# A vision-transformer layer with routed experts on one core: weights loaded for the expert stage, the last image's routing and the place of the weighing runs rearranged

## The chip, the cores and the metric

One core of a Trainium2 chip runs the whole kernel. The metric is the device time of one execution in microseconds. A difference of about 0.3% (5.6 us) is what a measurement of this kernel can tell from no change.

## The reference

Eight images of 3x512x512 become 8x1024 tokens of 256 values. One attention layer with eight heads and a gate follows, then a feed-forward layer whose down projection is chosen per token.

```python
h = patches @ Wp + bp + pos                      # [8, 1024, 256]
# attention on layernorm(h), 8 heads of 32; the softmax's rows are queries,
# and its result is used transposed
attn = softmax(q @ k.T * 32 ** -0.5)
out  = einsum('bhij,bhid->bhjd', attn, v) * sigmoid(x @ Wg.T + bg)
h = h + x + out @ Wf.T + bf                      # x is the normed input
# routed layer on layernorm(h)
H = gelu(xf @ W1 + b1)                           # 1024 wide
probs = softmax(H @ Wr + br); e = argmax(probs)
h = h + probs[e] * (H @ Wd[e] + bd[e])
```

## The kernel before

The images go through a pipeline on five engines, each with its own queue, and every order is written out by hand in the functions `image` of each engine; semaphores tie them together.

**An image** is 64 steps, `G_STEPS` = 32 for each group of four heads. Step k = 4i + hh takes query tile i and head hh: TensorE (PE) makes 128x1024 scores in two matmuls (L561), VectorE (DVE) their maximum (L1219), ScalarE (ACT) the exponential with its row sum (L930). Two score buffers are in turn, so score k waits for exponential k - 2. After the fourth head of a tile `scale_v` divides the values by the row sums (L1028, L1031), and `weigh(b, i, j)`, j = 0 to 3, adds the tile's product with its exponentials to the output (L575, 16 matmuls for two j). `WEIGH_AT` puts j = 0, 1 in step 4i + 5 and j = 2, 3 in step 4i + 7, at the step's end. Eight exponential buffers are in turn; exponential k waits for the weighing of the group eight steps before.

**Between the scores** of image b run, by tables `*_AT` of steps, the rest of the projections of b, the embedding of b + 1 (L528, into the two spare banks, added by `embedded` on DVE), gates, transposes (`turn`), the first projections of b + 1 (`QK0_AT`), and the routing of b - 1 (`route`, 14 small parts on DVE, one of them reading `prefix`, two products on PE that count the tokens of each expert, L674 and L676; project (0, 0) waits until its bank is read, L1146). The router layer of b - 1 (`norm_turn`, `router`, L625 to L643) stands whole at step 32.

**SyncE's queue** (SP) carries, in order for image b, `load_stack(b, 0)`, the tiles of image b + 1, `load_stack(b, 1)`, `store_hidden(b - 1, u)` for four quarters and `store_prob(b - 1)` (L312, after parts 8 and 9 of the routing). `load_stack` copies the split queries and keys of a group into `st`, three transfers per head, when the group before has made all its scores.

**The expert weights**, 16 pieces of 128x1024, come in three stages: `load_down(m)` (SP, L319, four transfers into one of four raw buffers), `high_down(m)` (ACT, L878, rounds) and `split_down(m)` (GpSimd, that is POOL, L417, the rest). Load m waits for split m - 4. In image 7 ACT rounds pieces 0 to 3 at steps 44, 48, 52, 56; 4 to 8 follow once the last weighing is done, and 9 to 15 stand inside the last router, behind every second gelu. SP loads 0 to 9, and then two more behind each `store_hidden(7, u)`, which waits for four transposed pieces of the hidden layer.

**The end.** After image 7's attention: final projection (L612), sums on DVE (L1047), statistics, `root_3` on POOL (L382), `norm_3` (L1058), transposes (L625), the router's 16 hidden pieces (L633 to L635) with gelu (L891), logits (L643, L650), `route(7)`, `place` (POOL, L409, eight scatters of token numbers into a table in DRAM), a gather of the table, and then 71 slots of 128 tokens through the experts (L791, L803), some 283 us. `bd_parts`, the two parts of the expert bias, go to `bd` by 16 transfers of 1 KB.

## Time and profile before

| | us |
|---|---|
| median of 3 runs | 1850.87 (1847.99 to 1852.8) |
| the profiled execution | 1851.56 |
| its span, first to last instruction | 1849.7 |
| PE busy | 1630.2 (88%) |
| DVE busy | 1165.1 (63%) |
| ACT busy | 940.0 (51%) |
| POOL busy | 369.2 (20%) |

The page also cuts the span into 40 slices of 46 us. PE's busy tenths are 9 in nearly all; the exceptions are slices 1, 2 and 4, then slices 28 to 34 (1248 to 1572 us) with 8, 8, 6, 7, 3, 4, 3, and the last one. The granted PE clock reads 8 to 9 tenths or more in all but slices 31 to 34, which read 7, 7, 6, 5. The last column of a wait, [idle before <- releaser], says how long the engine stood idle and what ended it.

### The profile page before, as it was taken

The page shows a single profiled execution, that of the slowest core. Times are in us where ns is not written, and L with a number is a line of the kernel's source. Part 1 is how long each engine was busy: PE and PEld are TensorE (multiplying, and loading weights), DVE is VectorE, ACT ScalarE, POOL GpSimd, SP SyncE. Part 2 cuts the span into 40 slices and gives each one's busy share as a digit, 9 for nine tenths or more (in the row PEclk, how much of TensorE's full clock was granted, in tenths as well). Part 3 has the DMA queues.
Part 4 walks back from the last instruction along what each step waited for, and adds up shares of the span by engine and source line. Part 5 has one row for each costly group of instructions (what it writes and reads, how often), then busy time and mean ns, then how long its engine had stood idle before and what let it go on. Part 6 is the DMA issues. An engine that isn't in the chain of part 4 may idle for free.

```text
span 1849.7 us, 29190 instructions
## 1 busy us (share of the span) xinstructions
PE 1630.2 (88%) x10992; PEld 1116.3 (60%) x10992; DVE 1165.1 (63%) x1977; ACT 940.0 (51%) x1565; POOL 369.2 (20%) x296
## 2 busy tenths in 40 slices
PE   7796999999999999999999999998867343999998
PEld 6463556456646655665566466644433232999998
DVE  2377687767777776768687777767656512444443
ACT  0465565756575666557565756565555121222222
POOL 0202001210210021001202100210003323455553
PEclk9898999999999999999999999999987765999999
DMA  4313325241604351352426043512443253566663
GB/s 164 86 52 69 64 79 131 47 109 52 160 2 117 81 122 31 104 123 64 95 66 142 19 109 79 133 24 69 106 91 56 71 111 104 176 201 203 205 200 136
DMA packets 131378, 187.45 MB, mean 101 GB/s; under 512 B 22222, under 2 KB 96476, under 8 KB 131116
## 3 DMA queue, kind: packets, MB, share of 16 engines
q1 hardware_dynamic: 112828, 120.48, 27.5%
q0 software_dynamic: 17984, 63.81, 10.7%
q8 instruction: 92, 1.51, 0.3%
q10 hardware_dynamic: 432, 1.31, 0.2%
q14 instruction: 42, 0.34, 0.1%
HBM read 84.44 MB, written 51.68 MB: 74 GB/s over the span
## 4 chain that ended last, share of the span: by engine, by line
PE 69%; DVE 12%; issue 8%; ACT 4%; DMA 3%; SPq 2%; POOL 1%; POOLq 0%; ACTq 0%; DVEq 0%
PE ps L561 12%; PE ps L803 11%; PE ps L575 11%; PE ps L528 8%; DVE nmax L1219 6%; PE ps L791 3%; PE ps L612 3%; PE ps L633 3%; PE ps L549 3%; ACT pr L930 3%; PE ps L635 3%; PE ps L634 3%; PE ps L588 3%; PE ps L595 1%; PE ps L502 1%
## 5 line engine op out<-in xcount | busy, mean ns | idle before, releaser
L1219 DVE TENSOR_REDUCE nmax<-ps 128x1 f32<-128x1024 f32 x512 | 622.8, 1219 | 231.9 <-PE ps L561 226.7
L930 ACT ACTIVATE pr<-ps,nmax 128x1024 f32<-128x1024 f32 x512 | 570.0, 1113 | 304.9 <-DVE nmax L1219 291.1
L561 PE MATMUL ps<-st 96*128 96x512 f32 x1024 | 404.0, 479 | 76.8 <-ACT pr L930 67.7
L561 PEld LDWEIGHTS ps<-st 96*128 96x128 f32 x1024 | 171.0, 194 | 275.8 <-ACT pr L930 137.5
L575 PE MATMUL ps<-pr,vs 128*32 128x256 f32 x4096 | 279.4, 394 | 18.4 <-DVE vs L1031 16.0
L803 PE MATMUL ps<-wd,hg 128*128 x1704 | 222.7, 287 | 0.0
L803 PEld LDWEIGHTS ps<-wd,hg 128*128 128x128 f32 x1704 | 210.0, 192 | 0.0
L575 PEld LDWEIGHTS ps<-pr,vs 128*32 128x32 f32 x4096 | 110.9, 111 | 163.7 <-issue 80.9
L962 ACT ACTIVATE hg<-ps 128x512 fp32r<-128x512 f32 x142 | 77.3, 595 | 226.7 <-PE ps L791 226.7
L528 PE MATMUL ps<-wp,xt 128*128 128x256 f32 x672 | 172.8, 379 | 0.0
L891 ACT ACTIVATE ht<-ps,bf 128x512 f32<-128x512 f32 x128 | 87.9, 688 | 125.3 <-PE ps L635 125.3
L549 PE MATMUL ps<-nt,wqk 128*128 128x512 f32 x256 | 135.2, 614 | 7.1 <-DVE base L1146 3.6
L528 PEld LDWEIGHTS ps<-wp,xt 128*128 128x128 f32 x672 | 126.3, 189 | 24.8 <-DVE qk L1019 1.2
L409 POOL DMA_INDIRECT slot_table<-tid,addr_i x64 | 63.2, 988 | 369.4 <-DVE addr_i L1157 352.4
L633 PE MATMUL ps<-nt_high,wf 128*128 128x512 f32 x256 | 106.7, 417 | 32.6 <-ACT ht L891 31.0
L1302 DVE TENSOR_TENSOR hg<-ps,hg 128x512 fp32r<-128x512 f32 x142 | 91.6, 686 | 48.4 <-ACT hg L962 48.2
L372 POOL TENSOR_SCALAR vare<-mv 128x8 f32<-128x8 f32 x8 | 1.9, 236 | 515.5 <-DVE mv L989 515.5
L1309 DVE SCALAR_TENSOR_TENSOR rows<-ps,rows 128x256 f32<-128x256 f32 x71 | 34.3, 484 | 110.1 <-PE ps L805 110.1
L634 PE MATMUL ps<-nt_low,wf 128*128 128x512 f32 x256 | 103.5, 404 | 0.0
L635 PE MATMUL ps<-nt_high,wf 128*128 128x512 f32 x256 | 103.3, 403 | 0.0
L930 ACT ACTIVATION_READ_ACCUMULATOR pr<-ps,nmax 128x1 f32 x512 | 99.5, 194 | 0.0
L469 POOL DMA_INDIRECT out<-rows,slot_to x71 | 69.9, 985 | 122.8 <-DVE rows L1309 113.9
(131 smaller groups left out, 1836.2 us busy)
## 6 DMA issues: line engine op xcount, KB each, us to landing
st<-qk SPq DMA_DIRECT2D x192, 256.0 KB, 5.1
xt<-x_in SPq DMA_DIRECT2D x58, 384.0 KB, 3.1
token_rows<-staged_b SPq DMA_DIRECT2D x64, 256.0 KB, 4.8
token_rows<-staged_a SPq DMA_DIRECT2D x64, 256.0 KB, 4.8
token_rows<-hres POOLq DMA_DIRECT2D x8, 1024.0 KB, 5.3
wd<-w_down SPq DMA_DIRECT2D x64, 128.0 KB, 4.4
pr<-x_in SPq DMA_DIRECT2D x6, 384.0 KB, 9.7
rows<-token_rows,slot_from POOLq DMA_INDIRECT x71, 4.7
```

Of the source, the lines that this page charges most:

```text
L528: last = mm(spare(t)[:, 0:D], xt[:, t % 2, k, :], wp[:, k, :], start=(k == 0), stop=(k == KC - 1))
L549: last = mm(spare(j), wqk[:, c, w * D + g * P:w * D + (g + 1) * P], nt[:, c, hf * HALF:(hf + 1) * HALF], start=(c == 0), stop=(c == DC - 1))
L561: last = mm(ps[:, 2 * (k % SR) + j, :], stq[:, hh, i * P:(i + 1) * P], stk[:, hh, j * 512:(j + 1) * 512], start=True, stop=True)
L575: last = mm(ps[32 * hh:32 * hh + 32, O_BANK + j // 2, (j % 2) * D:(j % 2 + 1) * D], vs[:, gi % 2, hh, :], pr[:, (4 * gi + hh) % PR, j * D: ...
L633: mm(spare(bank), w_high, nt_high[:, c, half], start=(c == 0), stop=False)
L634: mm(spare(bank), w_high, nt_low[:, c, half], start=False, stop=False)
L635: last = mm(spare(bank), w_low, nt_high[:, c, half], start=False, stop=(c == DC - 1))
L803: mm(o, hg[:, s % 2, h_part, k, :], wd[:, bass.ds(e, 1), w_part, k, :], start=(k == 0 and h_part == w_part), stop=False)
L891: actv(ht[:, k, :], spare(bank), ACT.Gelu, bias=bf1[:, k:k + 1]).then_inc(S["ff_act"], 1)
L930: actv(pr[:, k % PR, :], ps[:, 2 * (k % SR):2 * (k % SR) + 2, :].rearrange("p a n -> p (a n)"), ACT.Exp, bias=nmax[:, k % 16:k % 16 + 1], ...
L1219: V.reduce_max(nmax[:, k % 16:k % 16 + 1], ps[:, 2 * (k % SR):2 * (k % SR) + 2, :].rearrange("p a n -> p (a n)"), AX_X, negate=True).then_ ...
L1302: V.tensor_tensor(hg[:, s % 2, 1, 4 * c:4 * c + 4, :].rearrange("p k n -> p (k n)"), ps[:, 2 * (s % 2) + c, :], high_part.bitcast(F32), AL ...
```

## The change

- **Weighing.** `WEIGH_AT` moves each pair one step later (4i + 6 and 4i + 8, at the end of a group 30 and 31), and `weigh` stands right behind the step's score, ahead of the other work of the step.
- **Prefix.** One step later (step 48) and into spare bank 1 instead of 0; the wait for its reading moves from project (0, 0) at step 49 to project (1, 0) at step 52.
- **Stacks.** Head hh's transfers wait only for that head's last score, so that the first may go three steps earlier.
- **Weight pieces.** SP loads 0 to 3 ahead of `store_prob(6)`, 4 to 13 ahead of the first `store_hidden(7, 0)`, 14 and 15 behind it. POOL splits 0 and 1 ahead of `place(6)`, and 2 to 6 ahead of `root_3(7)`; 7 on follow it. ACT rounds 4 to 9 ahead of the last router, 10 behind its four roundings, 11 to 15 behind gelus 2, 4, 6, 8, 10.
- **Last image in two halves.** `route` takes a unit: images 0 to 6 whole, image 7 as units 7 and 8 of four tiles. Unit 7's parts run between the block transposes of the router's second half (`HALF_AT`), its `prefix` behind hidden piece 5, its `place` (four scatters) behind the last split. Unit 8 follows as the whole did, with one scan part less and four scatters.
- **Bias.** Its rounding moves to step 58 of image 7, its split ahead of split 2; it goes out to DRAM in one transfer and back into `bd` in one.

```diff
-        PREFIX_AT = G_STEPS + 15
+        PREFIX_AT = G_STEPS + 16
+        HALF_PREFIX = 5
+        HALF_AT = {0: (0, 1), 1: (2, 3), 2: (4, 5), 3: (6,), 6: (10, 11), 7: (12, 13)}
         WEIGH_AT = {k: [(i, j) for i in range(15) if i != 7 for j in range(4)
-                        if k == min(4 * i + 5 + j // 2 * 2, (i // TILES + 1) * G_STEPS - 1)] for k in range(STEPS)}
+                        if k == min(4 * i + 6 + j // 2 * 2, (i // TILES + 1) * G_STEPS - 2 + j // 2)] for k in range(STEPS)}
...
                 hold(sp, "qk_lo", b * 8 + 4 * (g + 1))
-                hold(sp, "score_mm", b * STEPS + g * G_STEPS)
                 for hh in range(4):
+                    wait(sp, "score_mm", b * STEPS + g * G_STEPS - 3 + hh)
...
-            for m in range(8):
+            for m in range(4):
                 load_down(m)
-            load_down(8)
-            load_down(9)
+            store_prob(IMAGES - 2)
+            for m in range(4, 8):
+                load_down(m)
+            sp.wait_ge(S["bd_low"], 1)
+            sp.dma_start(bd_rows.rearrange("a e d -> e a d"), bd_parts.bitcast(F32)).then_inc(S["bd_out"], 16)
+            for m in range(8, 14):
+                load_down(m)
             store_hidden(IMAGES - 1, 0)
-            load_down(10)
-            load_down(11)
-            store_hidden(IMAGES - 1, 1)
-            load_down(12)
-            load_down(13)
-            store_hidden(IMAGES - 1, 2)
             load_down(14)
             load_down(15)
-            store_hidden(IMAGES - 1, 3)
+            for u in range(1, 4):
+                store_hidden(IMAGES - 1, u)
             store_prob(IMAGES - 1)
-            for part in range(2):
-                for e in range(EXPERTS):
-                    sp.dma_start(bd[part:part + 1, e, :].bitcast(F32), bd_parts[e:e + 1, part, :].bitcast(F32)
-                                 ).then_inc(S["bd_in"], 16)
+            sp.wait_ge(S["bd_out"], 16)
+            sp.dma_start(bd[0:2].bitcast(F32), bd_rows).then_inc(S["bd_in"], 16)
...
+                if not after:
+                    split_down(0)
+                    split_down(1)
                 if before:
-                    place(b - 1)
+                    place(b - 1, b - 1, range(TILES))
             over_images(pool, image)
-            for m in range(4):
+            wait(pool, "bd_high", 1)
+            nc.gpsimd.tensor_tensor(bd_parts[:, 1], bd_raw, bd_parts[:, 0].bitcast(F32), ALU.subtract
+                                    ).then_inc(S["bd_low"], 1)
+            for m in range(2, 7):
                 split_down(m)
             root_3(IMAGES - 1)
             store_rear(IMAGES - 1, (IMAGES - 1) % 2)
-            for m in range(4, WD_PIECES):
+            for m in range(7, WD_PIECES):
                 split_down(m)
+            place(IMAGES - 1, IMAGES - 1, range(TILES // 2))
             pool.wait_ge(S["ff_mm"], 16 * IMAGES)
             nc.gpsimd.memset(bd[:].bitcast(F32), 0.0).then_inc(S["bd_zero"], 1)
-            place(IMAGES - 1)
+            place(IMAGES - 1, IMAGES, range(TILES // 2, TILES))
...
                     hidden(b, 1, k, 1 if k == 1 else k)
+                    if b == IMAGES - 1 and k == HALF_PREFIX:
+                        prefix(b, ps[:, 0, :])
...
                     score(b, k)
+                    for gi, j in WEIGH_AT[k]:
+                        weigh(b, gi, j)
...
                         if j == 0 and c == 0:
                             wait(pe, "tr_read", b * 8 + 16)
+                        if j == 1 and c == 0:
                             wait(pe, "r_read", b)
                         project(b + 1, 0, j, c)
                     if after and k in VALUE_AT:
                         values(b + 1, 0, VALUE_AT[k])
-                    for gi, j in WEIGH_AT[k]:
-                        weigh(b, gi, j)
...
+                if b == IMAGES - 1:
+                    high_down(10)
                 for hf in range(2):
...
-                        if b == IMAGES - 1 and k % 2 == 1 and HC * hf + k < 14:
-                            high_down(9 + (HC * hf + k) // 2)
+                        if b == IMAGES - 1 and k % 2 == 0 and 2 <= HC * hf + k <= 10:
+                            high_down(10 + (HC * hf + k) // 2)
...
+                    if not after and k == max(DOWN_AT) + 2:
+                        wait(act, "bd_raw_in", 16)
+                        actv(bd_parts[:, 0], bd_raw, ACT.Identity).then_inc(S["bd_high"], 1)
...
                     block_turn(last_b, hf, c)
+                    if hf == 1 and c in HALF_AT:
+                        for i in HALF_AT[c]:
+                            route(last_b, i)
...
-            for i in range(8):
-                route(last, i)
-            for i in (10, 11, 12, 13):
-                route(last, i)
-            for i in (8, 9):
-                route(last, i)
+            for i in (0, 1, 2, 3, 4, 5, 6, 10, 11, 12, 13, 8, 9):
+                route(last + 1, i)
```

## Rows read from the trace of the kernel before

**Rows 1.** Windows view, one stretch: busy us of each engine with (instructions), then PEclk, DMA share, GB/s.

```profile
740.00:920.00 180.00, 172.70 (x1119) 109.16 (x1119) 131.98 (x237) 106.78 (x178) 23.41 (x16) 1.00 0.40 97
```

**Rows 2.** Waits view, ACT from 1375 and PE from 1280 us, to 1570 us.

```profile
ACT wd L878 <- DMA wd<-w_down: 63.9, 5, 20.1
...
PE ps L633 <- ACT ht L891: 31.0, 3, 10.7
```

**Rows 3.** Waits view of PE, 200 to 1280 us: total us, times, longest.

```profile
PE ps L575 <- DVE vs L1031: 4.5, 9, 0.9
PE ps L549 <- DVE base L1146: 3.6, 6, 0.6
```

**Rows 4.** Timeline (start us, us, then [idle before <-releaser]), first half of image 7.

```profile
1299.44 0.17 DVE L1028 RECIPROCAL rinv<-rsum 128x4 f32<-128x4 f32 x1
...
1299.99 1.07 PE L575 MATMUL ps<-pr,vs 128*32 128x256 f32 x16 [0.36 <-DVE vs L1031]
...
1306.18 0.17 DVE L1028 RECIPROCAL rinv<-rsum 128x4 f32<-128x4 f32 x1
```

**Rows 5.** Timeline, DVE and POOL at step 32 of image 0.

```profile
157.32 1.28 DVE L1039 SCALAR_TENSOR_TENSOR gate<-gate,ps 128x512 f32<-128x512 f32 x2
157.49 4.50 POOL L389 TENSOR_TENSOR hres<-hres,a 128x2048 f32<-128x2048 f32 x1 [5.38 <-DVE a L995]
```

**Rows 6.** Timeline, step 44 of image 7.

```profile
1372.86 0.17 DVE L1028 RECIPROCAL rinv<-rsum 128x4 f32<-128x4 f32 x1
...
1376.69 0.38 SPq L312 DMA_DIRECT2D token_rows<-prob  x1
...
1383.53 1.06 ACT L878 ACTIVATE wd<-wd 128x1024 fp32r<-128x1024 f32 x1 [9.35 <-DMA wd<-w_down]
```

**Rows 7.** Timeline, last steps of image 7.

```profile
1407.36 0.17 DVE L1028 RECIPROCAL rinv<-rsum 128x4 f32<-128x4 f32 x1
...
1408.99 9.33 POOL L417 TENSOR_TENSOR wd<-wd 128x1024 fp32r<-128x1024 f32 x4
...
1414.55 3.93 DVE L1031 TENSOR_TENSOR vs<-v,rinv 128x128 f32<-128x128 f32 x1
...
1425.85 3.62 PE L575 MATMUL ps<-pr,vs 128*32 128x256 f32 x32 [2.35 <-DVE vs L1031]
...
1429.53 0.69 DVE L1039 SCALAR_TENSOR_TENSOR gate<-gate,ps 128x512 f32<-128x512 f32 x1 [3.74 <-PE ps L575]
```

**Rows 8.** Timeline and chain, from the last logits to the first expert rows.

```profile
1532.22 1.06 PE L650 MATMUL ps<-pick,xt 128*128 128x8 f32 x8 [0.81 <-DVE xt L1083]
...
1538.99 1.07 POOL L409 DMA_INDIRECT slot_table<-tid,addr_i  x1 [8.42 <-DVE addr_i L1157]
...
1548.03 7.39 DMA slot_table<-tid,addr_i
...
1567.44 1.94 PE L791 MATMUL ps<-ident,rows 128*128 128x128 f32 x8 [0.75 <-DMA rows<-token_rows,slot_from]
```

**Rows 9.** Timeline, from the last weighing to the last router's first matmul.

```profile
1444.39 15.56 DVE L1058 TENSOR_SCALAR n<-hres,mv,rstd 128x256 f32<-128x256 f32 x8 [2.20 <-POOL rstd L382]
...
1446.02 11.53 POOL L417 TENSOR_TENSOR wd<-wd 128x1024 fp32r<-128x1024 f32 x5
...
1465.06 0.50 PE L633 MATMUL ps<-nt_high,wf 128*128 128x512 f32 x1 [1.41 <-DVE nt_low L1068]
```

**Rows 10.** Chain view, matmuls behind the second such stall and a few us later.

```profile
1504.26 0.43 PE ps L634
...
1508.50 0.24 PE ps L633
```

**Rows 11.** Timeline, a weight piece behind a store, first of three times.

```profile
1475.89 5.67 SPq L319 DMA_DIRECT2D wd<-w_down  x8
1482.70 1.06 ACT L878 ACTIVATE wd<-wd 128x1024 fp32r<-128x1024 f32 x1 [11.04 <-DMA wd<-w_down]
```

**Rows 12.** DMA view: issues, median us to landing.

```profile
out<-rows,slot_to POOLq DMA_INDIRECT x71, 2.5
```

More of the change, by code:

```diff
@@ L331, in image @@
                         store_hidden(b - 1, u)
-                    store_prob(b - 1)
+                    if after:
+                        store_prob(b - 1)
             over_images(sp, image)
@@ L403, in _, with place @@
             nc.gpsimd.dma_start(rows_zero, zero).then_inc(S["table_in"], 16)
-            def place(b):
+            def place(b, unit, tiles):
                 wait(pool, "table_in", 16)
-                wait(pool, "addr_ready", b + 1)
-                for t in range(TILES):
+                wait(pool, "addr_ready", unit + 1)
+                for t in tiles:
                     nc.gpsimd.indirect_dma_start(
@@ L772, in _ @@
             turn_logits(IMAGES - 1, 1, 1)
-            wait(pe, "lg_done", 2 * IMAGES)
-            prefix(IMAGES - 1)
+            prefix(IMAGES, ps[:, 1, :])
             pe.wait_ge(S["tab_in"], 16)
@@ L948, in _ @@
             over_images(act, image)
-            act.wait_ge(S["bd_raw_in"], 16)
-            actv(bd_parts[:, 0], bd_raw, ACT.Identity).then_inc(S["bd_high"], 1)
-            for m in range(4, 9):
+            for m in range(4, 10):
                 high_down(m)
             router(IMAGES - 1)
-            exponentials(IMAGES - 1)
+            exponentials(IMAGES)
             act.wait_ge(S["wd_low"], WD_PIECES)
@@ L1134, in route @@
                 elif i == 8:
-                    wait(dve, "r_exp", r + 1)
+                    wait(dve, "r_exp", unit + 1 if whole else IMAGES)
                     link(V.reduce_sum(red[:, 2, :], ee[:], AX_X))
```

94 lines of the change are left out of this document (51 added, 43 removed).

## The prediction

> **What bounds the kernel now.** I read the page's slices first, then PE's windows and waits, then the timeline where slices fall. Up to image 6 PE is the bound: in one image it is busy 172.7 of 180 us at full clock [rows 1]. Nothing that only moves work can give much there, only the waits of PE that go. The slices are thin from 1341 us on, and there the reader should look for what PE waits for. ACT waits 63.9 us for weight pieces in five waits, and PE in turn 31.0 us for gelu in three [rows 2]. The expert stage behind it (from 1567 us) is not touched.
>
> **Images 0 to 6.** Two of PE's waits are addressed: the scaled values behind which a weighing stands, 4.5 us, and the reading of the prefix bank, 3.6 us, six times 0.6 [rows 3]. The weighing now comes a step after its values, and the prefix has a bank that is needed three steps later. Upper bound 8.1 us. The orders score, weigh, work and score, work, weigh have the same PE time in any two steps, and a score waits for the exponential of two steps before, so what is due next is that exponential; it will take back part. I take **5 us**; the bounds are a loss of 5 (0.1 us in each of 50 steps, a tenth of what a weighing lasts, 1.07 [rows 4]) and a gain of 8. The stacks per head I cost at nothing: no wait for them is among PE's between 200 and 1280 us; the work between the images and the router at step 32 hide them. In image 0, at step 32, there is no router, but the maximum on DVE stands behind the norms of image 1 and the gates, which end at 157.32 + 1.28 = 158.6 us [rows 5], so an earlier stack brings nothing there either. Were that cover gone, the head start of three steps would be the gain, some 3 x 1.7 us in image 0. Exponential k now waits for a weighing that follows score k by 1.07 us, while its own maximum takes 1.2, so this new wait is hidden by a tenth or two of a us.
>
> **Image 7 up to step 44.** No other work stands between the scores, so four steps take the chain's time: 1306.18 - 1299.44 = 6.74 us, and the weighing waits 0.36 us for its values [rows 4]. With that wait gone the next chain link is score, maximum, exponential. I take half of it, 0.18 x 11 groups = **2 us** (bounds 0 and 4).
>
> **Step 44 to the last weighing.** Here ACT meets piece 0 before it is there: SP issued it only behind the probabilities of image 6, at 1376.69, and ACT stood 9.35 us [rows 6]. Now loads 0 to 3 wait for the last gates alone, at step 38, six steps of 1.7 us or some 10 us earlier. They were in 6.8 us behind the store (1383.53 - 1376.69), so piece 0 is there before ACT's step 44. From the reciprocal of step 44 to the gate the old kernel took 1429.53 - 1372.86 = 56.7 us [rows 6, 7]. New: four groups with a rounding in each at 1414.55 - 0.2 (its reciprocal stands in front) - 1407.36 = 7.0 are 28; from the reciprocal of step 60 to that of the end about 6.2 (four steps less the scaling and its wait), then 0.5 for the scaling and 2.0 for two runs of weighing at full clock instead of 3.62 [rows 7]. That is 36.7. To it come holds of DVE by POOL's splits. The scaling at 1414.55 took 3.93 us, until POOL's four splits of 2.33 each were over [rows 7]. In the new order splits 2 and 3 wait for the bias at step 58 and run into the scaling of step 60 (take 2.5 us, between 0 and 4.7), split 1 may meet a routing part behind step 48 (1.0, between 0 and 2.3), the bias adds 0.4 on ACT. Sum 40.6, saved **16 us** (bounds 12 and 20).
>
> **From the gate to the experts.** The old way is 1567.44 - 1429.53 = 137.9 us [rows 7, 8]. The new one in terms:
> - Gate to the start of `norm_3`: 14.9, as before [rows 7, 9]. Splits 4 to 6 start behind ACT's rounding 1 us after the gate and last 7 us, so they end ahead of `root_3`, which is due after 12.7. The sums on DVE between them read PSUM and one SBUF tensor. At step 32 of image 0 two gate instructions of that kind, 1.28 us together, ran beside a POOL addition without any delay [rows 5], so I cost them at nothing.
> - `norm_3`: 15.56 before, because DVE stood still until POOL's five splits ended at 1457.55 [rows 9]. Now 7, 8 and 9 are left behind `root_3`: 0.9 for the store, 3 x 2.31, then 7 x 0.32 for the rest, 10.2. If 8 and 9 are not rounded by then, less (down to 2.6 if DVE gets in at once); if POOL finds more, 15.56.
> - To the router's first matmul: 1465.06 - 1459.95 = 5.1, as before.
> - Router to the second logits: 1532.22 - 1465.06 = 67.2 [rows 8, 9]. The three stalls, 31.0, go: pieces 10 to 13 no longer stand behind stores of the hidden layer. Behind each stall some nine matmuls ran 0.43 apart instead of 0.24 [rows 10], 28 x 0.19 = 5.3, which go with them. The prefix adds 1.1. Left: 32.0. Pieces 14 and 15 still stand behind `store_hidden(7, 0)`. In the old run such a piece was rounded 6.8 us after its load was begun [rows 11], and the store in front takes some 3.4. Counted out at 1.4 us a hidden piece (six matmuls of 0.24), the fourth is transposed 7.7 us into the router, so piece 14 is there at 17.9 and piece 15 at 20, while gelus 8 and 10 end at 16.8 and 20.7. So ACT stands 1.1 us once, beside PE's logits; I add 1.0 for this and for routing parts behind splits 13 to 15 (bounds 0 and 7).
> - Logits to the first scatter: 1538.99 - 1532.22 = 6.8, less 0.3 for the scan part that goes. POOL is free by then: its first `place` (four times 1.27) and the memory set of 1.8 us end about one us before.
> - Last scatter: 1548.03 - 1538.99 = 9.0 for seven gaps, now three, 3.9.
> - To the experts' first rows: 19.4, of it 7.39 until the table has landed [rows 8]. No row shows the landing of fewer scatters or without the bias's 16 transfers beside them; the lower end is 2.5, the landing of the later row scatters [rows 12]. I keep 7.39, the nearest row. The bias itself, one transfer instead of 16 (10 us of SP), is now clear of this path.
>
> Sum 14.9 + 10.2 + 5.1 + 33.0 + 6.5 + 3.9 + 19.4 = 93.0, saved **45 us** (bounds 33 and 54).
>
> **Total**: 5 + 2 + 16 + 45 = 68. The profiled execution took 1851.56, 0.7 over the median, so 1783.6 for it and **1783** for a median.
>
> **The rivals.**
> *Pieces are still late.* Loads 8 to 13 go through a ring of four, each behind a split that is itself behind a rounding. If POOL or SP falls a piece behind, one or two of the old stalls survive: 10.3 each and 1.8 for the slow matmuls behind, so 1795 or 1807. For it speaks that every piece's load is some 7 us long; against it that ACT needs one only every 2.8 us and has loads 8 to 10 in hand before `norm_3`. Chance 0.13.
> *POOL holds DVE.* Splits 13 to 15 meet routing parts of unit 7, which have two SBUF inputs like the scaling that was held: up to 3 x 2.3 on DVE, and the prefix on PE waits for them. That is 1789. Chance 0.10. The Trainium skill says as much: by "GPSIMD Engine Reference", Key points, the two engines share SBUF interfaces and contend where a DVE instruction has two SBUF inputs or runs in a two-port mode; by that rule the sums beside splits 4 to 6 are free and the routing parts are not, and the rows on the held scaling and the free gate agree with it.
> *More than that.* The table lands in 2.5 us and `norm_3` slips in between splits 7 and 8: 10 less, 1773. Chance 0.10.
> *Slower.* The weighing in front lengthens the step: what follows it (embedding, projection, transpose) reaches DVE or ACT 1.07 us later [rows 4]. Some 24 steps an image have both, 168 in seven images. If DVE or ACT stood for it and passed it on, 180 us at most; from 0.40 us a step it eats the 68. At half, 1873. Against it: the next maximum needs the next score, which stands behind the same work in PE's queue in either order. Chance 0.03.
> *Images 0 to 6 gain nothing*: 1788. It lies in the forecast's own spread.
>
> **How the numbers follow.** Forecast 0.64 (1774 to 1794 by its own terms), pieces late 0.13, holds 0.10, more 0.10, slower 0.03. The range of 1766 to 1806 takes in all but the slower case and the second surviving stall. Faster by over 0.3% (about what a measurement can tell) 0.96, within 0.3% 0.01, slower 0.03.
>
> **What would show it.** Right: in image 7 no wait of ACT for a piece at step 44; the span of an image shorter by under 1 us; `norm_3` around 10 us; no gap of PE over 2 us inside the last router, and its way to the second logits near 33 us; four scatters behind the last routing. Wrong: an L878 wait on w_down of over 5 us inside the router, L1128 or L1117 of 2 us or more, new waits of DVE for PE at L1004 or L1019 in images 1 to 6. The prediction fails as a whole if an image gets longer by over 5 us, or if PE idles for pieces as before.

## The result, and the profile after

| | before | after |
|---|---|---|
| median, us | 1849.51 (1847.99 to 1852.8, 4 runs) | 1787.45 (1786.31 to 1790.94, 4 runs) |
| the profiled execution, and its span | 1851.56, 1849.7 | 1790.94, 1789.1 |
| ratio of the times | | 0.9665 [0.9645, 0.9685] |

The change takes 62.1 us, 3.36% of the time. The kernel was run twice more, beside the experiments, where the kernel before took 1873.94 and 1872.71: 1800.29 (ratio 0.9613 [0.9597, 0.9629]) and 1799.47 (0.9605 [0.9587, 0.9623]). Chips differ by over 1%, so below only times of one group are compared, each with the kernel before of the same group.

The two traces cut at the same places (the gate's first instruction on DVE, the second logits, and so on) give the account of the 60.6 us between the spans:

| stretch | before, us | after, us | saved |
|---|---|---|---|
| start to the last `root_3` before image 7's | 1262.1 | 1259.3 | 2.8 |
| from there to the reciprocal of step 44 | 110.8 | 110.0 | 0.8 |
| to the gate | 56.7 | 43.0 | 13.7 |
| to the experts' rows | 137.9 | 95.4 | 42.5 |
| to the end | 282.3 | 281.5 | 0.8 |

The last mark but one is that of the prediction, 1567.44 before and 1507.64 after. It is the transposing of the second slot's rows; the first slot's stands at 1564.75 and 1503.41.

**Steady images.** The windows view, the stretch of [rows 1], has the same picture as before, PE busy 172.88 of 180 us:

```profile
740.00:920.00 180.00, 172.88 (x1118) 108.39 (x1117) 133.89 (x237) 106.47 (x177) 23.88 (x18) 1.00 0.40 94
```

PE's waits between 200 and 1280 us. The two of [rows 3], on the scaled values and on the prefix bank, are gone; a new one is there, the router's transposes (L630) on the last embedded rows (L1018). As before the change, by far the most is the wait for the exponentials:

```profile
PE ps L566 <- ACT pr L942: 31.9, 67, 1.3
PE ps L580 <- issue: 5.0, 2, 3.9
PE ps L648 <- ACT ht L903: 4.7, 6, 0.8
PE ps L630 <- DVE hres L1018: 3.1, 6, 0.5
```

An image can be halved in the trace by POOL's two square roots: `root_3` comes before the first half's work, `root_1` behind the router at step 32. Timeline of POOL, the kernel before (first half 988.30 - 920.38 = 67.92, second 101.99):

```profile
920.38 1.67 POOL L382 TENSOR_TENSOR rstd<-vare,half_neg 128x8 f32<-128x8 f32 x1
988.30 2.94 POOL L376 TENSOR_TENSOR rstd<-vare,half_neg 128x16 f32<-128x16 f32 x1
1090.29 1.68 POOL L382 TENSOR_TENSOR rstd<-vare,half_neg 128x8 f32<-128x8 f32 x1
```

And in the changed kernel (68.97 and 100.78):

```profile
919.76 1.67 POOL L383 TENSOR_TENSOR rstd<-vare,half_neg 128x8 f32<-128x8 f32 x1
988.73 2.93 POOL L377 TENSOR_TENSOR rstd<-vare,half_neg 128x16 f32<-128x16 f32 x1
1089.51 1.68 POOL L383 TENSOR_TENSOR rstd<-vare,half_neg 128x8 f32<-128x8 f32 x1
```

All six first halves are 67.91 to 67.93 before and 68.95 to 68.98 after: 1.04 us longer, without spread. The second halves, where the clock varies, take 103.0 in the mean of the last five before and 100.5 after.

**Image 7 to the gate.** ACT no longer stands at step 44 for piece 0. Timeline of the changed kernel: splits 2 and 3 (the first line) start 1.2 us before the scaling of step 60, which answers to the 3.93 of [rows 7]; the last weighing runs at half clock, as before; then the gate.

```profile
1397.00 4.66 POOL L418 TENSOR_TENSOR wd<-wd 128x1024 fp32r<-128x1024 f32 x2
...
1398.21 3.61 DVE L1045 TENSOR_TENSOR vs<-v,rinv 128x128 f32<-128x128 f32 x1
...
1408.55 3.64 PE L580 MATMUL ps<-pr,vs 128*32 128x256 f32 x32 [1.23 <-DVE vs L1045]
...
1412.26 1.29 DVE L1053 SCALAR_TENSOR_TENSOR gate<-gate,ps 128x512 f32<-128x512 f32 x2 [3.76 <-PE ps L580]
```

**The norm.** Three splits behind `root_3` instead of five, and `norm_3` is 5.3 us shorter than in [rows 9]:

```profile
1427.13 10.30 DVE L1072 TENSOR_SCALAR n<-hres,mv,rstd 128x256 f32<-128x256 f32 x8 [2.21 <-POOL rstd L383]
1428.06 6.94 POOL L418 TENSOR_TENSOR wd<-wd 128x1024 fp32r<-128x1024 f32 x3
```

**The last router.** Waits view of ACT from 1375 us; it answers to the 63.9 us of [rows 2]:

```profile
ACT wd L888 <- DMA wd<-w_down: 6.4, 3, 4.0
```

PE has no wait for gelu left but three of 2.5 us together. Inside the router there is one wait for a piece, 14, and two routing parts that stood beside splits:

```profile
1462.09 1.06 ACT L888 ACTIVATE wd<-wd 128x1024 fp32r<-128x1024 f32 x1 [1.05 <-DMA wd<-w_down]
...
1463.23 2.41 POOL L418 TENSOR_TENSOR wd<-wd 128x1024 fp32r<-128x1024 f32 x1 [4.61 <-ACT wd L888]
...
1464.40 1.29 DVE L1136 TENSOR_TENSOR oh_half<-oh_half,rnk 128x32 f32<-128x32 f32 x1
...
1465.92 2.41 POOL L418 TENSOR_TENSOR wd<-wd 128x1024 fp32r<-128x1024 f32 x1 [0.27 <-ACT wd L888]
...
1466.45 1.92 DVE L1142 TENSOR_TENSOR oh_half<-oh_half,red 128x32 f32<-128x32 f32 x1
```

**From the logits to the experts.** Timeline again. The cast of the addresses, some 0.17 us elsewhere, lasts 1.32 beside POOL's memory set; four scatters follow, the last at 1486.88:

```profile
1476.39 1.06 PE L655 MATMUL ps<-pick,xt 128*128 128x8 f32 x8 [0.81 <-DVE xt L1097]
...
1480.38 1.82 POOL L450 MEMSET bd<- 128x2048 f32 x1
...
1480.91 1.32 DVE L1178 CAST addr_i<-addr_f 128x4 int32<-128x4 f32 x1
...
1507.64 1.94 PE L801 MATMUL ps<-ident,rows 128*128 128x128 f32 x8 [2.29 <-DMA rows<-token_rows,slot_from]
```

and in the chain the landing of the last scatter, 7.39 us in [rows 8]:

```profile
1486.88 7.50 DMA slot_table<-tid,addr_i
```

### The profile page after: what moved, and what is told of

Same layout as the page of the kernel before. It is cut to its first block, busy times and chain, and to the rows that moved or that the text cites. A ratio compares the mean times of both kernels' runs of the same rounds, so it can differ in the third digit from the quotient of the medians.

```text
span 1789.1 us, 29203 instructions
## 1 busy us (share of the span) xinstructions
PE 1624.1 (91%) x10996; PEld 1107.0 (62%) x10996; DVE 1175.3 (66%) x1990; ACT 940.2 (53%) x1565; POOL 369.4 (21%) x296
## 4 chain that ended last, share of the span: by engine, by line
PE 69%; DVE 14%; issue 6%; ACT 6%; DMA 3%; SPq 1%; POOL 1%; POOLq 0%; ACTq 0%; DVEq 0%
PE ps L813 11%; PE ps L566 11%; PE ps L580 10%; PE ps L533 9%; DVE nmax L1240 7%; ACT pr L942 5%; PE ps L801 3%; PE ps L554 3%; PE ps L617 3%; PE ps L593 3%; PE ps L638 3%; PE ps L640 2%; PE ps L639 2%; PE ps L507 1%; PE ps L600 1%
## 5 line engine op out<-in xcount | busy, mean ns | idle before, releaser
L566 PE MATMUL ps<-st 96*128 96x512 f32 x1024 | 416.5, 490 | 70.6 <-ACT pr L942 64.7
L566 PEld LDWEIGHTS ps<-st 96*128 96x128 f32 x1024 | 178.8, 194 | 236.6 <-ACT pr L942 148.0
L533 PE MATMUL ps<-wp,xt 128*128 128x256 f32 x672 | 181.9, 393 | 0.0
L533 PEld LDWEIGHTS ps<-wp,xt 128*128 128x128 f32 x672 | 119.7, 189 | 53.2 <-issue 34.6
```

The costliest lines, as they stand in the source:

```text
L533: last = mm(spare(t)[:, 0:D], xt[:, t % 2, k, :], wp[:, k, :], start=(k == 0), stop=(k == KC - 1))
L566: last = mm(ps[:, 2 * (k % SR) + j, :], stq[:, hh, i * P:(i + 1) * P], stk[:, hh, j * 512:(j + 1) * 512], start=True, stop=True)
```

## The experiments

Three groups, each on one chip with the kernel before beside it. Three questions stood behind them: what the parts are worth apart, why first halves grew, and whether the holds of DVE by POOL are paid in the chain. What the traces show for the whole set, in us ("second half" is the mean of the last five; "44 to gate" starts with the reciprocal of step 44):

| kernel | first half | second half | 44 to gate | `norm_3` | gate to rows |
|---|---|---|---|---|---|
| before | 67.92 | 103.0 | 56.7 | 15.6 | 137.9 |
| after | 68.97 | 100.5 | 43.0 | 10.3 | 95.4 |
| group 1: e1 weighing only | 68.96 | 101.2 | 55.7 | 15.6 | 141.8 |
| e2 pieces only | 67.94 | 102.5 | 42.9 | 10.3 | 99.3 |
| e3 after, weighing undone | 67.94 | 101.1 | 43.1 | 10.3 | 95.0 |
| e4 after, image 7 routed whole | 68.97 | 100.7 | 41.1 | 10.3 | 98.5 |
| group 2: after again | 68.97 | 102.5 | 42.2 | 10.3 | 95.8 |
| e6 splits after the scaling | 68.97 | 101.7 | 40.8 | 10.3 | 95.4 |
| e7 splits after the norm | 68.97 | 102.1 | 42.5 | 2.9 | 87.2 |
| e8 step 31 weighed last | 68.18 | 102.4 | 45.1 | 10.3 | 96.7 |
| group 3: after, third time | 68.97 | 102.8 | 43.5 | 10.3 | 92.9 |
| e5 stacks only | 67.93 | 105.7 | 63.5 | 15.6 | 138.7 |
| e9 no holds | 68.97 | 102.1 | 40.8 | 2.9 | 85.9 |
| e10 no holds, step 31 weighed last | 68.18 | 103.2 | 41.6 | 2.9 | 86.6 |

Each row is one execution, and not always a typical one: those of e2, e4, e6, e7 and e9 are the fastest of their kernel, those of after, of its third time and of e10 the slowest. No trace of the kernel before was taken in the three groups, so a second half set against the 103.0 of "before" carries the chip with it. Within group 1, e2 can stand for the kernel before in images 1 to 6, since its edit touches only image 7.

### Group 1: the parts apart (the kernel before: 1858.82 us, 15 runs)

**e1, the weighing alone**: `WEIGH_AT` and the place of `weigh` in the kernel before.

```diff
-    if k == min(4 * i + 5 + j // 2 * 2, (i // TILES + 1) * G_STEPS - 1)]
+    if k == min(4 * i + 6 + j // 2 * 2, (i // TILES + 1) * G_STEPS - 2 + j // 2)]
...
                     score(b, k)
+                    for gi, j in WEIGH_AT[k]:
+                        weigh(b, gi, j)
...
-                    for gi, j in WEIGH_AT[k]:
-                        weigh(b, gi, j)
```

> The kernel before with the weighing alone moved (a step later, right behind the score). The forecast gave the weighing's part of images 0 to 6 some 2 to 3 us and image 7 some 2 us plus what its shorter steps bring, so about 4 us faster. The two traces say otherwise in one place: from the fourth root of an image to the next image's norm (67.65 us before) the changed kernel takes 68.7, a loss of 1.04 in each of seven images. If that loss is the weighing's, this kernel shows 68.7 there too, and its total is within 3 us of before (loss 7, gains 2 to 3 in the second halves and 3 to 5 in image 7). If the loss comes from the stacks, which now move inside the embedding, this kernel shows 67.65 and is 5 us faster or more.

Measured: 1852.6 us, ratio 0.9959 [0.9942, 0.9977]. Alone the weighing's place gives 6.2 us by the medians and 7.6 by the ratio, where the text on record expected the time within 3 us of the kernel before if the loss in the first halves was the weighing's. It is: they are 1.04 longer, here and in no kernel without this part. Second halves are 1.3 shorter than e2's, so an image gains 0.3 us; where the rest of the 6 to 8 us lies, no trace shows.

**e2, the weight pieces alone**: the order of loads, splits and roundings and the bias in one transfer, in the kernel before. The core of the edit:

```diff
-            for m in range(8):
+            for m in range(4):
                 load_down(m)
+            store_prob(IMAGES - 2)
+            for m in range(4, 8):
+                load_down(m)
...
-            for m in range(4):
+            for m in range(2, 7):
                 split_down(m)
             root_3(IMAGES - 1)
```

> The kernel before with the order of the weight pieces and the bias alone changed; weighing, prefix, stacks and the whole route of image 7 as before. By the forecast this is most of the gain: the stall at step 44 and its slow matmuls (13 of the 16), norm_3 (5.4), three stalls in the router with their slow matmuls (36.3), so some 53 us faster, 1797. The rival that the pieces are still late would leave one or two stalls of 10.3 us: 20 to 40 faster only.

Measured: 1801.26 us, ratio 0.9683 [0.9652, 0.9715]. This part carries the change: 57.6 us in this group, where 53 were expected. The stretch from step 44 to the gate is as short as in the changed kernel, and the way from the gate to the rows has all but 4 us of its gain.

**e3, the changed kernel with the weighing undone** (the edit of e1 backwards).

> The changed kernel with the weighing undone (old steps, at the end of the step). If the weighing costs 1.04 us in the first half of seven images and brings 2 to 3 in all second halves and 3 to 5 in image 7, this is within 4 us of the changed kernel, 1784 to 1791, and the first half of an image is 67.65 again. If the weighing brings the forecast's 4 us, it is 1791 or more.

Measured: 1788.92 us, ratio 0.9613 [0.9587, 0.964]. First halves are back at 67.94, second ones are 101.1 without the weighing's move. On this chip an ordinary image takes 67.94 + 101.12 = 169.06 without the move and, in e4 below, 68.97 + 100.66 = 169.63 with it. So what e1 gains alone is not there on top of the rest: set against e2's 102.5, the weighing shortens second halves by 1.3, the rest of the change by 1.4, both together by 1.8, and the weighing brings its 1.04 in the first halves. No kernel with the whole change ran on this chip, so no time settles what the move is worth on top of the rest. The nearest pair speaks against it: e4, which has the move and lacks the halves, is 8.5 us slower than e3, and the halves account for 3 to 4 of that.

**e4, the changed kernel with image 7 routed whole**: no `HALF_PREFIX`, no `HALF_AT`, one `place` of eight scatters behind the last routing.

```diff
-            place(IMAGES - 1, IMAGES - 1, range(TILES // 2))
...
-            place(IMAGES - 1, IMAGES, range(TILES // 2, TILES))
+            place(IMAGES - 1, IMAGES - 1, range(TILES))
```

> The changed kernel with image 7 routed in one piece behind the router, as before (eight scatters). By the forecast's terms the halves save 5.1 us of scatters and 0.3 of a scan part and cost 1.1 of prefix on PE; the trace of the changed kernel shows 2.0 us more in which PE waits for a routing part that DVE could not start beside POOL's splits. So this should be 1.5 to 4.5 us slower than the changed kernel, about 1790. If POOL's splits hold the route so long that the halves bring nothing, it is equal.

Measured: 1797.41 us, ratio 0.9661 [0.9636, 0.9685]. Gate to rows is 98.5 us, against 95.4 with halves in after and 95.0 in e3. From the transposes to the second logits it is 37.5 against 38.9, from there to the experts' first matmul (1.6 us behind the mark of the table) 37.3 against 32.8: the halves put 1.4 us into the router (their prefix on PE and its wait of 1.00 for a held part) and take 4.5 behind the logits. e2, which also routes whole, has 99.3. So the halves give 3 to 4 us.

### Group 2: the holds and step 31 (the kernel before: 1873.94 us, 11 runs)

**after again**, the yardstick.

> The changed kernel itself, as the yardstick of this group of runs, since chips differ by half a per cent. Both theories expect what was measured of it: a ratio to the kernel before of 0.966 (0.9645 to 0.9685), first halves of images 1 to 6 of 68.7 us and second halves of 100.3 to 101.1.

Measured: 1800.29 us, 0.9613 [0.9597, 0.9629]. The second halves are 2 us longer here (102.5), where 100.3 to 101.1 were expected. It is not the granted clock, 0.99 in the mean of these five halves in both traces; it is in the main one wait. The exponential of step 56 starts 1.2 us later than its maximum allows, in each of images 2 to 6, and PE stands 1.4 us for it. The timeline of ACT, the first run of this kernel and then this one:

```profile
549.12 1.11 ACT L942 ACTIVATE pr<-ps,nmax 128x1024 f32<-128x1024 f32 x1 [0.52 <-DVE nmax L1240]
```

```profile
549.48 1.11 ACT L942 ACTIVATE pr<-ps,nmax 128x1024 f32<-128x1024 f32 x1 [1.72 <-remote]
```

PE's waits between 200 and 1280 us have a line for it that the first run does not have:

```profile
PE ps L566 <- issue: 10.4, 11, 1.5
```

All changed kernels of groups 2 and 3 have this wait at step 56, 1.7 us or more, and e5 has one of 3.5 us there; after, the kernel before and group 1 do not have it. What it is stays open.

**e6, splits after the scaling.** One wait ahead of the bias's split, for the last scaling of image 7; the text on record calls the held scaling step 44's, but it is the one of step 60.

```diff
             wait(pool, "bd_high", 1)
+            wait(pool, "vs_ready", IMAGES * 16)
             nc.gpsimd.tensor_tensor(bd_parts[:, 1], ...
```

> The changed kernel with two waits added on GpSimd: the fill-in of the diagonals and splits 2 and on are let go only once VectorE has scaled step 44's values. In the trace of the changed kernel that scaling (line 1045) took 3.61 us beside the splits at 1397.00, against some 0.4 alone, and stands in the last image's own chain. Theory A (VectorE's two-input operation on SBUF stands still until GpSimd's run of splits ends, and the chain pays for all of it): the scaling takes 0.3 to 0.5 us, the stretch from step 44's reciprocals to the gate's logits falls from 43.0 to 39 to 41 us, and the time falls by 1.5 to 3.5 us against the changed kernel. Theory B (the held scaling only uses up time in which something else, the loads or TensorE's half clock, would have been waited for): the scaling is short, but the stretch stays at 42 to 43 and the time within 1 us of the changed kernel. Rival C (the splits now run later, into the norm and the router, and hold something there): the stretch shortens and the norm or the router lengthens by as much, time equal or up to 3 us longer.

Measured: 1794.25 us, 0.9584 [0.957, 0.9598], 6.0 us under the yardstick. Timeline of the yardstick: the scaling held until the splits end.

```profile
1405.48 4.65 POOL L418 TENSOR_TENSOR wd<-wd 128x1024 fp32r<-128x1024 f32 x2
...
1407.89 2.40 DVE L1045 TENSOR_TENSOR vs<-v,rinv 128x128 f32<-128x128 f32 x1
```

Timeline of e6: the scaling free, and five splits from 1410.96 on, beside the last weighing and the gate, which they do not touch.

```profile
1403.26 0.29 DVE L1046 TENSOR_TENSOR vs<-v,rinv 128x128 f32<-128x128 f32 x1
...
1410.18 3.51 PE L581 MATMUL ps<-pr,vs 128*32 128x256 f32 x32 [2.09 <-DVE vs L1046]
...
1413.73 1.28 DVE L1054 SCALAR_TENSOR_TENSOR gate<-gate,ps 128x512 f32<-128x512 f32 x2 [3.61 <-PE ps L581]
```

The hold of 2.11 us is paid in full where it stands. From the reciprocal of step 60 to the last one it is 8.79 us in the yardstick and 6.57 in e6, and it was 10.00 in after, where the hold took 3.32. The whole stretch shows only 42.2 - 40.8 = 1.4, since the four steps ahead of it happen to take 9.67 in e6 and 8.76 in the yardstick: PE stood there 2.44 us and 1.03 us with no named releaser, at the steps where this chip adds its wait. The rest of the 6.0 is not the hold's. In the traces 5.8 us lie in images 1 to 6, which the edit cannot reach, and 1.8 between gate and norm, where the granted clock was 0.81 in the yardstick and 0.96 in e6; the final projection takes 9.03 and 7.17 us. I took that for a consequence of the hold until group 3: there the changed kernel, held, has the short 14.9 us from gate to norm and the unheld e10 the long 16.7. So the clock in that stretch changes between executions, and nothing ties it to the hold. Theory A stands, at some 2 us: the three unheld kernels e6, e9 and e10 take 40.8 to 41.6 us from step 44 to the gate, the eight held ones with the new loads 42.2 to 45.1, but for e4 with 41.1.

**e7, splits after the norm.** One wait ahead of split 7, for the normed values.

```diff
+            wait(pool, "xn_ready", IMAGES)
             for m in range(7, WD_PIECES):
                 split_down(m)
```

> The changed kernel with waits added on GpSimd ahead of split 7, so that splits 7 to 9 start only once VectorE has written the normed values that step 47's norm needs (line 1072, 10.30 us there in the changed kernel, beside splits at 1428.06). Theory A (the hold is GpSimd's and lies in the chain): norm_3 takes 2.5 to 3.5 us and the time falls by 6 to 8 us against the changed kernel, unless the splits that are moved back hold something in the router: then 4 to 7 us. Theory B (norm_3 is long of its own accord, as a strided operation with two inputs): it stays at 9 to 10.5 us and the time does not fall. What is late next under A: the routing's own parts beside splits 7 to 12, which held 1.3 to 1.9 us in the changed kernel, and may hold up to 3.5 more.

Measured: 1791.83 us, 0.957 [0.9555, 0.9584], 8.5 us under the yardstick. Timeline: `norm_3` takes 2.94 and the splits come behind it.

```profile
1436.53 2.94 DVE L1073 TENSOR_SCALAR n<-hres,mv,rstd 128x256 f32<-128x256 f32 x8 [2.21 <-POOL rstd L383]
...
1439.56 9.32 POOL L418 TENSOR_TENSOR wd<-wd 128x1024 fp32r<-128x1024 f32 x4 [2.11 <-DVE n L1073]
```

The 7.36 us between 10.30 and 2.94 are the hold, and all of it was in the chain; gate to rows is 8.6 us shorter than in the yardstick. Nothing else took its place: the norm's end to the second logits is 41.9 less 3.0 = 38.9 us, as in after. The gain left lying by the change is thus larger than the one it made in this norm.

**e8, step 31 weighed last**, the first halves' own question.

```diff
-                    for gi, j in WEIGH_AT[k]:
-                        weigh(b, gi, j)
+                    if k != G_STEPS - 1:
+                        for gi, j in WEIGH_AT[k]:
+                            weigh(b, gi, j)
...
                         embed(b + 1, t, part)
+                    if k == G_STEPS - 1:
+                        for gi, j in WEIGH_AT[k]:
+                            weigh(b, gi, j)
```

> The changed kernel, but in each image's first half the last embedding's pieces are issued ahead of the weighing of the same step, as in the kernel before; everywhere else the weighing stays right behind the scores. Theory A (the 1.04 us that each first half lengthened come from the last embedding, which with the new order ends last on TensorE, so that the transposes behind it wait for VectorE's write of the embedded rows, line 630 on line 1018): the first halves go back from 68.7 to 67.6 to 67.9 us, the second halves stay at 100.3 to 101.1, and the time falls by 5 to 8 us against the changed kernel (0.8 to 1.0 for each of seven or eight halves). Theory B (the 1.04 us come from the step's other edits, or from the weighing displacing work in all of the half's steps): first halves stay at 68.3 to 68.7 and the time within 1.5 us.

Measured: 1798.3 us, 0.9583 [0.9565, 0.9602]. One of its six executions took 4659.87 us and is in this median but not in the ratio; that of the other five is 1797.3, 3.0 under the yardstick. The ratios are 5.6 us apart, with overlapping intervals. The trace is plainer than the times. Timeline of the changed kernel at step 31, from its first run: weighing, then the last embedding, then DVE's write of it, and the transposes wait for that.

```profile
978.28 1.07 PE L580 MATMUL ps<-pr,vs 128*32 128x256 f32 x16
979.28 1.13 PE L533 MATMUL ps<-wp,xt 128*128 128x256 f32 x4
980.45 0.42 DVE L1018 TENSOR_TENSOR hres<-ps,posb 128x256 f32<-128x256 f32 x1 [0.84 <-PE ps L533]
...
980.93 1.97 PE L630 MATMUL ps<-ident,n 128*128 128x128 f32 x16 [0.52 <-DVE hres L1018]
```

Timeline of e8: the weighing covers the write, and the transposes wait for nothing.

```profile
981.83 1.03 PE L533 MATMUL ps<-wp,xt 128*128 128x256 f32 x4
982.79 1.07 PE L580 MATMUL ps<-pr,vs 128*32 128x256 f32 x16
983.17 0.41 DVE L1022 TENSOR_TENSOR hres<-ps,posb 128x256 f32<-128x256 f32 x1
...
983.79 1.97 PE L630 MATMUL ps<-ident,n 128*128 128x128 f32 x16
```

All six first halves are 68.17 to 68.20: 0.79 of the 1.04 us come back, 4.7 in all, and not in seven or eight halves as the text on record has it, since image 0 has no router at step 32 and image 7 no embedding at step 31. Theory A holds for three quarters of the 1.04. What the last 0.25 are, no run settles. The second halves, expected at 100.3 to 101.1, have this chip's 102.4.

### Group 3: together (the kernel before: 1872.71 us, 13 runs)

**after, third time**, the yardstick.

> The changed kernel once more, as the yardstick of this group of runs: a ratio to the kernel before of 0.961 to 0.967, by the two groups so far.

Measured: 1799.47 us, 0.9605 [0.9587, 0.9623], a hair below what was expected.

**e5, the stacks alone**, in the kernel before.

```diff
-                hold(sp, "score_mm", b * STEPS + g * G_STEPS)
                 for hh in range(4):
+                    wait(sp, "score_mm", b * STEPS + g * G_STEPS - 3 + hh)
```

> The kernel before with one thing of the change: the four stacks of a half image are let go head by head, each once the last scores of its own head have been issued, where they all waited for the last scores of the half. Theory A (as the prediction put it: the stacks were in time already, and no wait of TensorE on them is in the trace of the kernel before): time within 2 us of the kernel before, first halves unchanged at 67.7 (times the chip's own factor). Rival B (the earlier transfers are what makes second halves shorter by 1 to 3 us in the changed kernel, or what lengthens the first ones by 1.04): second halves 101 to 102 instead of 104, time 8 to 15 us less, or first halves 68.7.

Measured: 1873.23 us, ratio 1.0005 [0.9993, 1.0018]; first halves 67.93. The stacks head by head are worth nothing. The second halves are 105.7, not the 101 to 102 of rival B; they have this chip's wait at step 56 in them.

**e9, no holds**: e6 and e7 together, the diagonals' zeroing ahead of the first `place`, and piece 14 ahead of the first hidden stores.

```diff
-            place(IMAGES - 1, IMAGES - 1, range(TILES // 2))
             pool.wait_ge(S["ff_mm"], 16 * IMAGES)
             nc.gpsimd.memset(bd[:].bitcast(F32), 0.0).then_inc(S["bd_zero"], 1)
+            place(IMAGES - 1, IMAGES - 1, range(TILES // 2))
...
-            store_hidden(IMAGES - 1, 0)
             load_down(14)
+            store_hidden(IMAGES - 1, 0)
             load_down(15)
```

> The changed kernel with all of the holds on VectorE by GpSimd taken out of the last image's chain: splits 2 and on wait for step 44's scaling, splits 7 to 9 for the normed values, the zeroing of the diagonals stands ahead of the last scatters instead of in VectorE's last parts, and piece 14 is loaded ahead of the first hidden stores. Theory A (each hold is paid in the chain, and the pause ahead of the gate costs TensorE's clock too): the two gains measured alone, 6.0 and 8.5 us, add up, and the zeroing and the load give 0.5 to 1.5 more: 14 to 16 us less than the changed kernel of this group, norm_3 at 2.7 to 3.2 us, no two-input SBUF operation of VectorE over 0.4 us in the chain from step 44 on. Theory B (the splits are only put off and become late themselves, so that the experts or the loads wait): 5 to 10 us less, and a wait of ScalarE's or the experts' on a weight piece that is not in the trace of the changed kernel.

Measured: 1789.23 us, 0.956 [0.9542, 0.9578], 10.2 under the yardstick, less than the 14 to 16 expected. By stretches of the traces the norm gives 7.4 and the way from step 44 to the gate 2.7, together 10.1 (gate to rows as a whole gives 7.0: the zeroing brings 1.1 there, and what follows the last scatter takes 1.4 more); the sum expected had taken e6's 6.0 whole, of which some 2 were the hold. The two traces alone would have misled: their spans are 16.0 us apart, but 5.0 of that lie ahead of step 44, and they are the fastest execution of e9 and the slowest of its yardstick. The zeroing does what it was moved for:

```profile
1473.03 1.06 PE L657 MATMUL ps<-pick,xt 128*128 128x8 f32 x8 [0.81 <-DVE xt L1099]
...
1477.62 0.17 DVE L1180 CAST addr_i<-addr_f 128x4 int32<-128x4 f32 x1
...
1482.45 0.97 POOL L410 DMA_INDIRECT slot_table<-tid,addr_i  x1 [0.30 <-issue]
```

The cast takes 0.17, and from the second logits to the last scatter it is 9.4 us instead of 10.5. But from the logits to the experts' first matmul e9 takes 30.5 and its yardstick 30.2, since what follows the scatter (the landing and two gathers) varies by more than the 1.1: 22.4 us in after, 19.7 in the yardstick, 21.1 in e9. Theory B's late pieces are not there: ACT's list of waits from 1270 us on has none for a weight piece. But the kernel is not without holds, as theory A has it. The last two splits now start right ahead of two routing parts, which stand for a whole split each, and both are in the chain that ended last:

```profile
1458.81 2.40 DVE L1135 TENSOR_TENSOR oh_half<-rl,red 128x32 f32<-128x32 f32 x1
...
1462.67 2.33 DVE L1144 TENSOR_TENSOR oh_half<-oh_half,red 128x32 f32<-128x32 f32 x1
```

From the transposes to the second logits e9 takes 39.0 us, its yardstick 39.0 and after 38.9, so they cost the router no more than the shorter ones of the changed kernel.

**e10, no holds and step 31 weighed last.**

> The kernel of the run before this one (no holds in the last image's chain) and, in each image's first half, the last embedding ahead of the weighing of step 31, as tried alone before, where first halves came down by 0.78 us each and the median by 2 us. Theory A: the two add: 3 to 6 us less than without it, 17 to 21 less than the changed kernel. Theory B (what the half gains is given back to TensorE's clock, as the run alone left open with 2 us of the 5 to 8 expected): within 2 us of the kernel without it, first halves shorter by 0.8, later stretches longer at a lower granted clock.

Measured: 1784.64 us, 0.9524 [0.9502, 0.9545], 14.8 us under the changed kernel and 88 under the one before, the fastest of all. Against e9 it is 4.6 us by the medians and 6.7 by the ratios; with e8's 5.6 these are two readings of the same edit, beside 4.7 by the first halves, six times 0.79. So that the two edits add is borne out by two pairs of kernels, with overlapping intervals in each; the 17 to 21 us under the changed kernel were not reached, as e9's 14 to 16 were not. Theory B is not ruled out: in the two traces e10's first halves are 4.7 us shorter in all and its images 1 to 6 are 3.8 longer, though e10's is the slowest of its four executions and e9's the fastest.

## Why the prediction was right, and where its terms were off

The time, 1787.45, lies 4.5 us above the forecast of 1783 and inside the range. It was taken from 68 us of savings where the traces show 60.6 and the medians 62.1, so the mechanisms named there carry the result, and no large error was made good by another. By its own steps:

- **Images 0 to 6: 5 predicted, 2.8 measured, and in part by luck.** The two waits went, as said. But the term missed a cost and undersized a gain, and a chance event hid the rest. The cost: 1.04 us in each of six first halves, of which 0.79 are a new wait of the router's transposes for the last embedding (e1, e3, e8). The step that failed is "the orders score, weigh, work and score, work, weigh have the same PE time": true for the steps, but at the end of a half the work behind the weighing is what the next stage waits for. The prediction's rival on this ("what follows it reaches DVE or ACT 1.07 us later") named the mechanism; it happens once in a first half and not in 24 steps an image. Its own list of signs of being wrong had "new waits of DVE for PE at L1004", and the changed kernel has them: DVE's embedding sum (now L1018) waits 30 times for PE between 200 and 1280 us, 15.9 us in all, and never before; most of these cost nothing. The gain: 2.5 us in each second half, where 0.5 and 0.6 were allowed for the two waits. By e2 (102.5), e3 (101.1) and e5 (no time gained) the prefix's new place is the likely source of 1.4 of it, but no run had it alone. An ordinary image is 1.5 us shorter in all, more than the "under 1 us" named as a sign of being right. The chance event: a pause of PE at 390 us (below), 3.93 us after and 2.21 before, with a lower clock behind it, makes one image 4.2 us longer.
- **The stacks at nothing**: right (e5).
- **Image 7 to step 44: 2 predicted, 0.8 measured.** Where nothing else runs, four steps now take 6.57 or 6.58 us instead of 6.74, which is the half of the 0.36 that was taken. That gave 1.0 by step 32; behind it the granted clock was lower, 0.79 against 0.93 in the last 18 us, and took 0.2 back.
- **Step 44 to the gate: 40.6 us predicted, 43.0 measured.** The stall of ACT is gone and the routing part beside split 1 took 1.29 us, as foreseen. Off are the scaling, held 3.3 us beyond its 0.29 where 2.5 were taken, and the last weighing, 3.64 us at half clock where 2.0 were taken. "At full clock instead of 3.62" was an assumption without a row: of 14 traces two have less than 3.4, e10 with 2.69 and e3 with 1.93.
- **Gate to rows: 93.0 predicted, 95.4 measured.** Term by term: gate to norm 14.9 and 14.9; `norm_3` 10.2 (its own terms add up to 10.1) and 10.3; to the first matmul 5.1 and 5.2; to the second logits 33.0 and 33.8; to the first of the last scatters 6.5 and 6.7, with 1.15 lost to the zeroing that was thought to be over by then and some 1.0 gained elsewhere; scatters 3.9 and 3.8; to the rows 19.4 and 20.8. Of the last, the landing is 7.50 against 7.39, and the gather of the second slot's rows 7.39 against 6.02. One pair says little here: over all traces the landing is 7.4 to 8.8 us behind eight scatters (five kernels) and 6.0 to 8.1 behind four (nine traces), 8.1 and 7.0 in the mean. Fewer scatters may shorten it by 1 us; the bias beside them makes no difference that shows (8.36 and 8.07 without its 16 transfers, 7.39 to 8.83 with them).
- **The holds' rival** came true in part. Routing parts stood 1.29 and 1.92 us, just short of the 2 us named as a sign of being wrong, and PE waited once 1.00 for it; it was priced at 6. In e9 and e10, where the splits start right ahead of two parts, these stand 2.3 to 2.4 us each. The Trainium skill, "GPSIMD Engine Reference", Key points, has the contention tied to the shared SBUF interfaces, with DVE instructions that have two SBUF inputs or a two-port mode. The rows agree for the scaling, the routing parts and the free gate; the cast and `norm_3`, held too, have one tensor input in SBUF, and that they are of its second kind is not shown by any row here.
- **Late pieces**: one wait of 1.05 us inside the router, 1.1 foreseen. **More than that**: the landing stayed at 7.50, and `norm_3` waited for all three splits. **Slower**: see the first point.

What bounded the gain was foreseen by its mechanism, but I did not ask what it would take to avoid it: I costed the norm's hold at 7.6 us and kept it, and e7 shows that a wait of one line gets it back.

## What to carry to other kernels

- A split or copy on GpSimd that nobody needs yet should stand behind the operation of VectorE that the chain is waiting for, by a wait if need be: one line gave 8.5 us here, of which 7.4 are the hold's in the trace.
- When a block of PE's work moves ahead of another, look at what stands last in front of the next stage. The same order that is free inside a stage costs, at its end, the answer time of the engine behind it.
- Parts that each remove the same wait do not add: the weighing's place gave 6 to 8 us alone and, in the images of group 1, nothing on top of the rest. And a gain of 2 to 6 us measured in one pair should be looked for in the stretch that was edited before it is added to another.

## What the runs showed of the hardware

- **A held operation of VectorE mostly waits for the whole run of GpSimd's, not for one instruction.** All scalings and norms that met splits ended within 0.2 us of the last split: 3.61 us beside two splits (from 1398.21 to 1401.82, splits until 1401.66), and in `norm_3` only the first of eight instructions stood (8.03 us), the other seven took 0.32 each. But a routing part of 128x32 was let go between two splits that follow each other without a gap, in e8 (below; the first split ends at 1475.52) and in the changed kernel's third run. What decides it no run shows.

```profile
1473.12 4.75 POOL L418 TENSOR_TENSOR wd<-wd 128x1024 fp32r<-128x1024 f32 x2 [5.20 <-ACT wd L892]
...
1474.29 1.27 DVE L1140 TENSOR_TENSOR oh_half<-oh_half,rnk 128x32 f32<-128x32 f32 x1
```

- **A memory set on GpSimd holds even a cast** of 128x4 elements (1.32 us instead of 0.17); the reduction behind it shows 1.24 instead of 0.21, but it may only have queued.
- **One pause of PE for which the profile names no cause.** In 13 of 14 executions PE stood at 390 to 397 us inside a run of weighing, for 2.2 to 5.7 us with "issue" as the releaser, whatever the kernel; e5's has no such pause there. Where it was long the granted clock fell behind it. Windows view, 390 to 400 us, the kernel before and the changed one:

```profile
390.00:400.00 10.00, 7.79 (x64) 6.81 (x61) 2.55 (x4) 1.20 (x2) 0.00 (x0) 1.00 0.88 214
```

```profile
390.00:400.00 10.00, 6.07 (x46) 4.20 (x46) 1.28 (x2) 1.08 (x2) 0.00 (x0) 0.66 0.66 182
```

What it is stays open.
- **The gain depends on the chip**: 62 us on one and 73 on another, where the kernel before is 1.3% slower and the changed one 0.7%. The first halves take the same 67.93 and 68.97 us everywhere; it is second halves and image 7 that differ. In the second halves it is in the main the wait at step 56; in image 7, step 44 to the gate takes e5 63.5 us where the kernel before took 56.7, while the changed kernel has 42.2 to 43.5 on both chips.
